# A second buffer for the softmax scales, GpSimd's scaling placed earlier, and V's last products placed earlier

## The chip, the cores and the metric

The kernel runs on one core of a Trainium2 chip. A core has a matrix engine (TensorE, PE in the profile; PEld is its weight load), a vector engine (VectorE, DVE), a scalar engine (ScalarE, ACT), a general engine (GpSimd, POOL) and an engine that mostly issues transfers (SyncE, SP). Each works through its own list of instructions in order and waits on semaphores. The metric is device time in microseconds; lower is better.

## The reference

One layer of a gated cross-attention block with a mixture of experts. B = 4 sequences of S = 512 tokens, width 256, 16 heads of 16:

```python
x = x + jnp.tanh(g_xattn[0]) * _L0_xattn_ref(_layernorm(x, axis=-1), ctx_1024, ctx_1024, ...)
x = x + jnp.tanh(g_ffn[0]) * _L0_ffn_ref(_layernorm(x, axis=-1), ...)
```

```python
q = _split_heads(Q @ Wq.T + bq)
k = _split_heads(K @ Wk.T + bk)
v = _split_heads(V @ Wv.T + bv)
scores = jnp.einsum('bhqd,bhkd->bhqk', q, k) * scale
attn = jax.nn.softmax(scores, axis=-1)
ctx = jnp.einsum('bhqk,bhkd->bhqd', attn, v)
...
return ctx @ Wo.T + bo
```

The second half (`_L0_ffn_ref`) routes every token to the 2 best of 8 experts, adds a shared expert, and is not touched by the change.

## The kernel before

**Attention in groups.** Attention runs over 16 groups (`GROUPS`): a group `i` is one sequence and four heads. A group has four steps (`kt`, 128 keys each). In a step TensorE makes four score tiles (`scores`, line 1621), four tiles of scores for the row maxima of a later group (`scores_for_max`, line 1387), and the products of the weights with V for the step before (`values`, line 1500). ScalarE takes the exponentials (line 816) and copies the products out (`sums_copy`, line 802). VectorE reduces the maxima (line 939). GpSimd adds the four partial sums of a group (`add_part`, line 679, three per group).

**How a group gets its maxima.** The row maxima are subtracted inside the score product, as extra rows of `QS`. For group i+1 they are finished in the first step of group i. Then GpSimd splits them (`split_max`, lines 589 and 591), VectorE transposes them (line 947), GpSimd copies them (`max_rows`, line 602, semaphore `m_ready`), and SyncE loads them (`load_max`, line 404, `QK<-mparts` in the rows). TensorE can't begin group i+1 before that load has landed (`m_in`).

**SyncE's list.** SyncE works in passes; pass i goes with group i. It issues `load_group(i+3)`: twelve transfers of 64 KB (lines 394 and 397) with the queries and keys of a later group. The first four wait until group i-1's scores are done, the other eight wait until the first step of group i has its exponentials (`exp_done`). Then come `load_max(i+1)`, `load_sums(i-1)` (line 409), `store_scale(i-2)` (line 413) and `load_scale(i-3)` (line 420). After pass 12 there is no `load_group`; in passes 12 to 14 weights of the second half follow.

**The scales.** For the first 14 groups the softmax division works on the transposed context: denominators go out by `load_sums`, VectorE takes reciprocals, `store_scale` writes them to memory and `load_scale` reads them back, each row repeated 16 times, into `SCALES` (the space of V's weights, `w_v` in the rows). One `SCALES` buffer holds two groups, and GpSimd multiplies two groups of context by it at once (`scale_context(n)`, line 633, for groups 2n and 2n+1, semaphore `ctx_scaled`). `load_scale(i)` waits until `ctx_scaled` reaches i // 2, so the pair before must have been multiplied.

**GpSimd's list.** In its iteration i: the last addition of group i-1, `split_max(i+1)`, `max_rows(i+1)`, `pack_out(i-1)` (four transfers, line 354), an addition of a bias to one tile of X (line 668), the first addition of group i, in odd iterations from 5 on `scale_context((i-5)//2)`, and the second addition of group i. It reaches these about a third of a group to a whole group after TensorE began group i.

**The first steps.** V of the last sequence is made inside the first two steps of group 0: `last_value_rows(kt, 0)` after the first pair of maxima tiles and `last_value_rows(kt, 1)` after the second pair (line 1485), and ScalarE copies it out after the fourth exponential of the step (`v_copy`, line 733). The score tiles, V's products and the sums share four banks in turn, so the score tile four turns after a V tile waits for that copy.

Of the kernel before, what the change touches and what calls it, by code (L numbers as in the profile page):

```python
# [6 lines left out]
ALU = mybir.AluOpType  # L7
# [8 lines left out]
def flamingo_layer(nc, x, ctxT, g_xattn, g_ffn, WqT, bq, WkT, bk, WvT, bv, WoT, bo,  # L16
# [3 lines left out]
    DK = D // H  # L20
# [46 lines left out]
    with ExitStack() as stack:  # L67
# [65 lines left out]
        SCALE = sb("SCALE", [P, 2, G * TB])  # L133
        SCALES = W["v"][:, :, :].rearrange("p c d -> p (c d)")
        CTX = CH[:, :, :].rearrange("p t d -> p (t d)")[:, 24:24 + TURNED // 2 * S].rearrange("p (n s) -> p n s", s=S)
# [89 lines left out]
        den_in, scale_out = sems("den_in", 2), sems("scale_out", 2)  # L225
        scale_ready, scale_in, ctx_scaled = sem("scale_ready"), sems("scale_in", 2), sem("ctx_scaled")

# [129 lines left out]
        def _(sp):  # L357
# [57 lines left out]
            def load_scale(i):  # L415
                sp.wait_ge(scale_out[i % 2], times(i))
                if i == 0:
                    sp.wait_ge(v_done, 2 * B)
                wait(sp, ctx_scaled, i // 2)
                sp.dma_start(SCALES[64 * (i % 2):64 * (i % 2 + 1), :],  # L420
                             r_scr[i].unsqueeze(1).to_broadcast([G, DK, S])).then_inc(scale_in[i % 2], 16)

# [119 lines left out]
        def _(pool):  # L542
# [85 lines left out]
            def scale_context(n):  # L628

                for h in range(2):  # L630
                    pool.wait_ge(ctx_in[h], 16 * G * (n + 1))
                    pool.wait_ge(scale_in[h], 16 * (n + 1))
                nc.gpsimd.tensor_tensor(CTX[:, n, :], CTX[:, n, :], SCALES, ALU.mult).then_inc(ctx_scaled, 1)

# [46 lines left out]
            for i in range(TURNED + 1):  # L681
                if i:
                    add_part(i - 1, 3)
                split_max(i + 1)
                max_rows(i + 1)
                if i:
                    pack_out(i - 1)
                else:
                    bias_x(range(4))
                if i < 12:  # L690
                    bias_x(range(4 + i, 5 + i))
                add_part(i, 1)
                if i >= 5 and i % 2:
                    scale_context((i - 5) // 2)
                if i < TURNED:
                    add_part(i, 2)
# [26 lines left out]
        def _(act):  # L723
# [84 lines left out]
            for i in range(GROUPS):  # L808
                for kt in range(TB):
                    for j in range(G):  # L810
                        act.wait_ge(st_done[j % 2], G // 2 * (TB * i + kt) + j // 2 + 1)
                        if i:
                            act.wait_ge(pv_done, TB * (i - 1) + kt + 1)
                        if i == 0 and kt == 2 and j == 2:
                            act.wait_ge(v_done, 2 * B)
                        nc.scalar.activation(PT[:, kt, j, :], PS[:, ring_bank("score", TB * i + kt, j), :], ACT.Exp).then_inc(exp_done, 1)  # L816
                        n = TB * i + kt - TAIL
                        if j == 3 and n in (2, 4):
                            h2t_first(n // 2 - 1)
                    if i == 0 and kt < 2:  # L820
                        v_copy(B - 1, PS[:, ring_bank("v", kt), :], kt)
                    if TB * i + kt:
# [531 lines left out]
        def _(pe):  # L1354
# [250 lines left out]
            for i in range(GROUPS):  # L1605
# [18 lines left out]
                for kt in range(TB):  # L1624
                    pairs = pairs_at(i, kt)
                    scores(kt, 0)
                    scores(kt, 1)
                    for n in pairs[0:1]:
                        scores_for_max(n)
                        scores_for_max(n + 1)  # L1630
                    if i == 0 and kt < 2:
                        last_value_rows(kt, 0)
                    scores(kt, 2)
# [235 lines left out]
```

## Time and profile before

| | |
|---|---|
| median of 3 runs | 471.99 us (471.62 to 473.8) |
| the profiled execution | 474.82 us, of which the span of the profile is 472.6 us |
| TensorE busy | 440.2 us (93%) |
| VectorE busy | 315.0 us (67%) |
| ScalarE busy | 267.2 us (57%) |
| GpSimd busy | 223.1 us (47%) |

Times in the rows are microseconds from the start of the span. 2.2 us of the profiled execution lie outside the span. A busy TensorE is not TensorE at its full rate; the granted clock (PEclk) is 1.00 at 2.4 GHz and 0.50 at 1.2 GHz.

### The profile page before, as it was taken

To read this page: it belongs to the slowest core of one execution; us is meant where nothing else is said; L and a number is where in the kernel's file an instruction comes from. 1 tells how busy PE (TensorE), PEld (TensorE's weight loads), DVE (VectorE), ACT (ScalarE), POOL (GpSimd) and SP (SyncE) were. 2 spreads that over 40 slices of the span, in tenths; PEclk is the share of its full clock that TensorE was granted. 3 is DMA by queue.
4 is the path that set the end of the run, shared out by engine and by line. 5 is a ranking of instruction groups with operands and counts; after the bars stand their busy time and mean duration, and the time that the engine had idled before them with its cause. 6 is when DMAs were issued, how large, how long until landed. Compare 5 with 4: busy or idle time off the path is not lost.

```text
span 472.6 us, 8388 instructions
## 1 busy us (share of the span) xinstructions
PE 440.2 (93%) x2294; PEld 225.8 (48%) x2294; DVE 315.0 (67%) x719; ACT 267.2 (57%) x564; POOL 223.1 (47%) x345
## 2 busy tenths in 40 slices
PE   8999999999969979495999999999999999999997
PEld 7654444333323323132355464575555555555745
DVE  1976938999866959394837877555665656542574
ACT  2545439999977959395864611113666667631110
POOL 5335525877863939384654476750333233322000
PEclk9999969999997989798999999999999999999999
DMA  8689561334362434327082582241323223211931
GB/s 259 242 238 295 172 234 53 90 97 106 84 115 64 89 89 82 76 65 144 19 242 86 157 289 91 101 121 49 90 81 91 83 88 91 81 56 48 359 112 60
DMA packets 45500, 58.93 MB, mean 125 GB/s; under 512 B 12496, under 2 KB 25680, under 8 KB 45456
## 3 DMA queue, kind: packets, MB, share of 16 engines
q1 hardware_dynamic: 38864, 46.05, 35.0%
q0 software_dynamic: 4960, 10.53, 7.1%
q10 hardware_dynamic: 1632, 1.84, 1.2%
q8 instruction: 19, 0.31, 0.3%
q14 instruction: 25, 0.20, 0.2%
HBM read 36.35 MB, written 19.81 MB: 119 GB/s over the span
## 4 chain that ended last, share of the span: by engine, by line
PE 64%; ACT 8%; DMA 8%; DVE 7%; issue 7%; SPq 6%; POOL 0%; ACTq 0%; DVEq 0%; POOLq 0%
PE PS L1665 11%; PE PS L1776 9%; ACT R L816 7%; PE PS L1500 6%; DMA QK<-mparts 6%; PE PS L1678 6%; PE PS L1621 5%; PE PS L1795 5%; PE PS L1440 4%; PE PS L1387 4%; PE PS L1771 3%; PE PS L1547 3%; SPq L397 2%; SPq L394 2%; PE PS L1790 2%
## 5 line engine op out<-in xcount | busy, mean ns | idle before, releaser
L939 DVE TENSOR_REDUCE nmax<-PS 128x2 f32<-128x1024 f32 x114 | 134.2, 1214 | 42.0 <-PE PS L1387 40.5
L816 ACT ACTIVATE R<-PS 128x512 f32<-128x512 f32 x256 | 134.3, 630 | 37.3 <-PE PS L1621 36.8
L1621 PE MATMUL PS<-QK 50*128 50x512 f32 x256 | 84.1, 475 | 22.5 <-DMA QK<-mparts 21.2
L679 POOL TENSOR_TENSOR R<-R 128x512 f32<-128x512 f32 x48 | 61.6, 1284 | 43.6 <-ACT R L802 42.0
L1621 PEld LDWEIGHTS PS<-QK 50*128 50x128 f32 x256 | 37.4, 197 | 83.4 <-ACT R L816 38.7
L1500 PE MATMUL PS<-R 128*32 128x512 f32 x512 | 72.6, 639 | 2.5 <-ACT R L816 1.6
L718 POOL DMA_INDIRECT token_y<-R,dest x34 | 32.6, 959 | 86.7 <-DVE R L1270 86.4
L1387 PE MATMUL PS<-QK 48*128 48x512 f32 x256 | 61.6, 458 | 1.3 <-DVE nmax L925 0.9
L1776 PE MATMUL PS<-R 128*128 x100 | 47.3, 595 | 0.2 <-ACT R L884 0.2
L831 ACT ACTIVATE R<-PS 128x512 f32<-128x512 f32 x16 | 9.6, 597 | 60.6 <-PE PS L1665 60.6
L802 ACT COPY R<-PS 128x512 f32<-128x512 f32 x64 | 38.6, 603 | 7.5 <-PE PS L1500 7.0
L1387 PEld LDWEIGHTS PS<-QK 48*128 48x128 f32 x256 | 29.3, 200 | 22.1 <-DVE nmax L939 13.1
L640 POOL DMA_INDIRECT slot_x<-CH,pos x32 | 31.1, 973 | 10.8 <-issue 8.4
L1308 DVE TENSOR_TENSOR R<-R,PS 128x256 f32<-128x256 f32 x34 | 14.3, 421 | 32.4 <-ACT R L881 27.2
L1665 PE MATMUL PS<-R,wgate 128*128 128x512 f32 x64 | 30.4, 597 | 0.0
L1665 PE MATMUL PS<-R,wup 128*128 128x512 f32 x64 | 30.3, 595 | 0.0
L881 ACT ACTIVATE R<-PS 128x256 f32<-128x256 f32 x34 | 13.0, 383 | 30.1 <-PE PS L1776 27.3
L354 POOL DMA_DIRECT2D CH<-R x56 | 27.8, 501 | 4.2 <-POOL mparts L602 4.2
L1678 PE MATMUL PS<-wdown,R 128*128 128x256 f32 x128 | 28.9, 380 | 0.0
L1678 PEld LDWEIGHTS PS<-wdown,R 128*128 128x128 f32 x128 | 24.0, 190 | 4.4 <-issue 1.4
L1776 PEld LDWEIGHTS PS<-R 128*128 128x128 f32 x100 | 18.7, 190 | 14.3 <-issue 13.1
L1795 PE MATMUL PS<-fc,R 128*128 x100 | 25.6, 380 | 0.0
(181 smaller groups left out, 621.5 us busy)
## 6 DMA issues: line engine op xcount, KB each, us to landing
QK<-q_parts SPq DMA_DIRECT2D x96, 64.0 KB, 2.8
QK<-k_parts SPq DMA_DIRECT2D x96, 64.0 KB, 2.9
k_parts<-R SPq DMA_DIRECT2D x8, 512.0 KB, 4.0
q_parts<-R SPq DMA_DIRECT2D x8, 512.0 KB, 4.8
R<-in_fc_w_dram SPq DMA_DIRECT2D x16, 256.0 KB, 5.1
R<-token_y SPq DMA_DIRECT2D x4, 1024.0 KB, 9.1
R<-slot_x SPq DMA_DIRECT2D x25, 129.0 KB, 2.1
fc<-in_fc_w_dram SPq DMA_DIRECT2D x16, 128.0 KB
```

What stands on the lines that cost most here:

```text
L679: nc.gpsimd.tensor_tensor(OT[i % 2], OT[i % 2], PART[kt - 1], ALU.add).then_inc(summed, 1)
L718: nc.gpsimd.indirect_dma_start(token_y, bass.IndirectOffsetOnAxis(ap=dest[:, j:j + 1], axis=0), YE[:, j % UN, :], None).then_inc(y_out[j % ...
L802: nc.scalar.copy(PART[kt - 1] if kt else OT[i % 2], PS[:, ring_bank("sums", n), :]).then_inc(sums_out, 1)
L816: nc.scalar.activation(PT[:, kt, j, :], PS[:, ring_bank("score", TB * i + kt, j), :], ACT.Exp).then_inc(exp_done, 1)
L939: nc.vector.tensor_reduce(nmax[:, i % 2, at:G * TB:G * TB // 2], PS[:, smax_bank(n):smax_bank(n) + 2, :], AX.X, ALU.max, negate=True).then ...
L1387: mm(PS[:, smax_bank(n), :], QS[g][at, h, qt * P:(qt + 1) * P], KST[g][at, h, :], start=True, stop=True).then_inc(smax_done[n % 2], 1)
L1500: last = mm(PS[32 * j:32 * j + VW, ring_bank("sums", n), :], VA[:, b * TB + kt, (g * G + j) * VS:(g * G + j) * VS + VW], PT[:, kt, j, :], ...
L1621: mm(PS[:, ring_bank("score", TB * i + kt, j), :], KST[g][at, h, kt * P:(kt + 1) * P], QS[g][at, h, :], start=True, stop=True).then_inc(st ...
L1665: last = mm(PS[:, gu_bank(n, k), :], w[:, d, c * P:(c + 1) * P], H2T[:, d, b * S:(b + 1) * S], start=(d == 0), stop=(d == DC - 1))
L1678: last = mm(PS[:, down_bank(b, t), half * D:(half + 1) * D], HS[:, b % 2, c, t * P:(t + 1) * P], wdown[:, c, :], start=(c == 0 and half == ...
L1776: last = mm(PS[:, 1 + u, :], XGT[:, u, c * P:(c + 1) * P], fc1[:, c, e, :], start=(c == 0), stop=(c == DC - 1))
L1795: last = mm(PS[:, 5 + u, 0:D], HET[:, u, c * P:(c + 1) * P], fc2[:, c, e, :], start=(c == 0), stop=(c == IE // P - 1))
```

## The change

Three edits. `SCALES` becomes two buffers, the space of V's weights and that of Q's weights, used in turn by pairs of groups; `load_scale(i)` waits for one pair less (`ctx_scaled` at i // 2 - 1) and once for Q's last product; `scale_in` has four semaphores. GpSimd's `scale_context` stands ahead of the bias addition and of `add_part(i, 1)`. In the first two steps of group 0, V's first products stand ahead of the first pair of maxima tiles, and ScalarE's copy of V stands ahead of the fourth exponential.

```diff
-        SCALES = W["v"][:, :, :].rearrange("p c d -> p (c d)")
+        SCALES = [W[n][:, :, :].rearrange("p c d -> p (c d)") for n in "vq"]
...
                 sp.wait_ge(scale_out[i % 2], times(i))
                 if i == 0:
                     sp.wait_ge(v_done, 2 * B)
-                wait(sp, ctx_scaled, i // 2)
-                sp.dma_start(SCALES[64 * (i % 2):64 * (i % 2 + 1), :],
-                             r_scr[i].unsqueeze(1).to_broadcast([G, DK, S])).then_inc(scale_in[i % 2], 16)
+                if i == 2:
+                    sp.wait_ge(qk_done, 4 * B)
+                wait(sp, ctx_scaled, i // 2 - 1)
+                sp.dma_start(SCALES[i // 2 % 2][64 * (i % 2):64 * (i % 2 + 1), :],
+                             r_scr[i].unsqueeze(1).to_broadcast([G, DK, S])).then_inc(scale_in[i % 4], 16)
...
-                    pool.wait_ge(scale_in[h], 16 * (n + 1))
-                nc.gpsimd.tensor_tensor(CTX[:, n, :], CTX[:, n, :], SCALES, ALU.mult).then_inc(ctx_scaled, 1)
+                    pool.wait_ge(scale_in[2 * (n % 2) + h], 16 * (n // 2 + 1))
+                nc.gpsimd.tensor_tensor(CTX[:, n, :], CTX[:, n, :], SCALES[n % 2], ALU.mult).then_inc(ctx_scaled, 1)
...
+                if i >= 5 and i % 2:
+                    scale_context((i - 5) // 2)
                 if i < 12:
                     bias_x(range(4 + i, 5 + i))
                 add_part(i, 1)
-                if i >= 5 and i % 2:
-                    scale_context((i - 5) // 2)
...
                     for j in range(G):
+                        if i == 0 and kt < 2 and j == 3:
+                            v_copy(B - 1, PS[:, ring_bank("v", kt), :], kt)
...
-                    if i == 0 and kt < 2:
-                        v_copy(B - 1, PS[:, ring_bank("v", kt), :], kt)
...
                     scores(kt, 1)
+                    if i == 0 and kt < 2:
+                        last_value_rows(kt, 0)
                     for n in pairs[0:1]:
                         scores_for_max(n)
                         scores_for_max(n + 1)
-                    if i == 0 and kt < 2:
-                        last_value_rows(kt, 0)
```

SyncE's list at the end of pass 5, with the waits in brackets (`o_scales` is the memory that holds the scales, `w_v` and `w_q` are the two buffers). Before:

```order
L404 DMA QK<-mparts 2x8x128
L409 DMA DENS<-R 128x1x16 [waits summed]
L413 DMA o_scales<-SCALE 128x16 [waits scale_ready]
L420 DMA w_v<-o_scales 64x1x512 [waits ctx_scaled,scale_out0]
L394 DMA QK<-q_parts 16x2x512 [waits st_done1,st_done0]
```

and after:

```order
L404 DMA QK<-mparts 2x8x128
L409 DMA DENS<-R 128x1x16 [waits summed]
L413 DMA o_scales<-SCALE 128x16 [waits scale_ready]
L422 DMA w_q<-o_scales 64x1x512 [waits qk_done,scale_out0]
L394 DMA QK<-q_parts 16x2x512 [waits st_done1,st_done0]
```

No transfer has moved in SyncE's list; the load of the scales no longer waits for GpSimd there.

GpSimd's list in its iteration 5, from the copies of the maxima on. Before:

```order
L602 COPY mparts<-mturned 32x32 x4
L354 DMA CH<-R 16x512 x4
L668 TENSOR_TENSOR X<-X,tg_bo 128x256
L679 TENSOR_TENSOR R<-R 128x512
L633 TENSOR_TENSOR CH<-CH,w_v 128x512
L679 TENSOR_TENSOR R<-R 128x512 x2
L589 CAST nmax_parts<-nmax 128x16
```

and after:

```order
L604 COPY mparts<-mturned 32x32 x4
L354 DMA CH<-R 16x512 x4
L635 TENSOR_TENSOR CH<-CH,w_v 128x512
L670 TENSOR_TENSOR X<-X,tg_bo 128x256
L681 TENSOR_TENSOR R<-R 128x512 x3
L591 CAST nmax_parts<-nmax 128x16
```

The multiplication has moved ahead of the bias addition and of one addition; nothing was added to the iteration.

TensorE's list in the first two steps of group 0 (1621 or 1623 are scores, 1387 or 1389 maxima tiles, 1485 or 1487 V). Before:

```order
L1621 MATMUL PS<-QK 128x512 x2
L1387 MATMUL PS<-QK 128x512 x2
L1485 MATMUL PS<-w_v,R 128x256 x2
L1621 MATMUL PS<-QK 128x512
L1387 MATMUL PS<-QK 128x512 x2
L1485 MATMUL PS<-w_v,R 128x256 x2
L1621 MATMUL PS<-QK 128x512 x3
L1387 MATMUL PS<-QK 128x512 x2
L1485 MATMUL PS<-w_v,R 128x256 x2
L1621 MATMUL PS<-QK 128x512
```

and after:

```order
L1623 MATMUL PS<-QK 128x512 x2
L1487 MATMUL PS<-w_v,R 128x256 x2
L1389 MATMUL PS<-QK 128x512 x2
L1623 MATMUL PS<-QK 128x512
L1389 MATMUL PS<-QK 128x512 x2
L1487 MATMUL PS<-w_v,R 128x256 x2
L1623 MATMUL PS<-QK 128x512 x3
L1487 MATMUL PS<-w_v,R 128x256 x2
L1389 MATMUL PS<-QK 128x512 x2
L1623 MATMUL PS<-QK 128x512
```

In both steps the first V products have changed places with the first pair of maxima tiles.

## Rows read from the trace of the kernel before

**Rows 1.** Page, part 4: shares of the chain that ended last, by line.

```profile
PE PS L1665 11%; PE PS L1776 9%; ACT R L816 7%; PE PS L1500 6%; DMA QK<-mparts 6%; PE PS L1678 6%; PE PS L1621 5%; PE PS L1795 5%; PE PS L1440 4%; PE PS L1387 4%; PE PS L1771 3%; PE PS L1547 3%; SPq L397 2%; SPq L394 2%; PE PS L1790 2%
```

**Rows 2.** Waits: who waited for whom, us in total, times, longest; SyncE's own last.

```profile
PE PS L1621 <- DMA QK<-mparts: 21.2, 6, 5.9
SPq L250 <- POOL CH L633: 13.9, 5, 3.2
```

**Rows 3.** Timeline of TensorE, first score tiles of groups 6, 7, 9, 11, 13.

```profile
127.79 0.51 PE L1621 MATMUL PS<-QK 50*128 50x512 f32 x2 [0.88 <-DMA QK<-mparts]
142.65 0.79 PE L1621 MATMUL PS<-QK 50*128 50x512 f32 x2 [4.81 <-DMA QK<-mparts]
168.46 0.55 PE L1621 MATMUL PS<-QK 50*128 50x512 f32 x2 [3.91 <-DMA QK<-mparts]
195.55 0.79 PE L1621 MATMUL PS<-QK 50*128 50x512 f32 x2 [5.94 <-DMA QK<-mparts]
222.19 0.80 PE L1621 MATMUL PS<-QK 50*128 50x512 f32 x2 [5.26 <-DMA QK<-mparts]
```

**Rows 4.** Windows: groups 0; 1 to 5; 7; 6 to 13; half clock; 5.

```profile
core 0: us, PE busy (x) PEld busy (x) DVE busy (x) ACT busy (x) POOL busy (x), PEclk, DMA share, GB/s
56.30:76.49 20.19, 18.12 (x74) 7.94 (x71) 11.29 (x13) 11.15 (x22) 7.24 (x13) 0.75 0.45 152
76.49:127.79 51.30, 49.64 (x324) 19.00 (x321) 48.47 (x50) 50.60 (x102) 38.57 (x70) 1.00 0.39 99
142.65:154.48 11.83, 11.83 (x64) 4.55 (x64) 8.93 (x10) 9.62 (x19) 5.19 (x13) 0.76 0.26 67
127.79:233.78 105.99, 85.56 (x512) 32.41 (x512) 75.85 (x80) 80.01 (x159) 64.22 (x115) 0.89 0.41 83
62.90:73.20 10.30, 10.30 (x35) 4.62 (x36) 3.34 (x4) 4.22 (x9) 4.27 (x9) 0.50 0.60 219
116.85:127.79 10.94, 9.97 (x68) 3.86 (x65) 10.11 (x11) 10.62 (x22) 8.61 (x15) 1.00 0.42 101
```

**Rows 5.** Timeline of SyncE in passes 3 and 4 (no wait for `ctx_scaled`).

```profile
105.90 0.56 SPq L420 DMA_DIRECT2D w_v<-o_scales  x1
113.63 1.12 SPq L404 DMA_DIRECT2D QK<-mparts  x2
```

**Rows 6.** Timeline of SyncE in passes 5 and 7 to 8.

```profile
121.51 1.96 SPq L394 DMA_DIRECT2D QK<-q_parts  x1
...
153.21 0.48 SPq L413 DMA_DIRECT2D o_scales<-SCALE  x1
157.00 0.56 SPq L420 DMA_DIRECT2D w_v<-o_scales  x1
...
163.23 1.11 SPq L404 DMA_DIRECT2D QK<-mparts  x2
```

**Rows 7.** The chain that ended last, in order of time: start, us, what.

```profile
125.50 2.24 DMA QK<-mparts
136.01 6.59 DMA QK<-mparts
163.81 4.60 DMA QK<-mparts
```

**Rows 8.** Timeline of GpSimd: iterations 5, 5 to 6, 8, and its last multiplication.

```profile
127.84 1.27 POOL L633 TENSOR_TENSOR CH<-CH,w_v 128x512 f32<-128x512 f32 x1
...
130.94 1.30 POOL L679 TENSOR_TENSOR R<-R 128x512 f32<-128x512 f32 x1 [0.58 <-ACT R L802]
...
160.35 0.98 POOL L602 COPY mparts<-mturned 32x32 f32<-32x32 f32 x4 [0.31 <-DVE mturned L947]
...
264.83 1.28 POOL L633 TENSOR_TENSOR CH<-CH,w_v 128x512 f32<-128x512 f32 x1 [6.87 <-DMA w_v<-o_scales]
```

**Rows 9.** Timeline of group 0's first two steps: TensorE's two idle times.

```profile
57.65 0.50 PE L1387 MATMUL PS<-QK 48*128 48x512 f32 x2 [0.91 <-DVE nmax L925]
...
62.52 0.50 PE L1621 MATMUL PS<-QK 50*128 50x512 f32 x1 [1.16 <-ACT R L733]
```

More of the change, by code:

```diff
@@ L225, in flamingo_layer @@
         den_in, scale_out = sems("den_in", 2), sems("scale_out", 2)
-        scale_ready, scale_in, ctx_scaled = sem("scale_ready"), sems("scale_in", 2), sem("ctx_scaled")
+        scale_ready, scale_in, ctx_scaled = sem("scale_ready"), sems("scale_in", 4), sem("ctx_scaled")
         ct_t, wo_done, x1_ready = (sem(n) for n in ("ct_t", "wo_done", "x1_ready"))
```

## The prediction

> **What bounds the kernel now.** First the chain that ended last, summed by line [rows 1]: TensorE has most of it, but 6% of the span stands under the load of a group's maxima, and 6% of 472.6 is 28 us in which no engine computes on the chain. Next the waits [rows 2]: TensorE's score product waited 21.2 us for that load, in 6 waits, and SyncE itself was held for 13.9 us, in 5 waits, by GpSimd's multiplication with the scales. Then TensorE's timeline shows where [rows 3]: 0.88 us at group 6, then 4.81, 3.91, 5.94 and 5.26 us at groups 7, 9, 11 and 13, together 19.92 us for the last four. Every second group stalls, and GpSimd multiplies in every second of its iterations. Last the windows [rows 4]: groups 1 to 5 took 51.30 us, 10.26 each; groups 6 to 13 took 105.99 us. A group without a stall takes 142.65 - 4.81 - 127.79 = 10.05 us [rows 3]. So eight groups cost 105.99 - 8 x 10.05 = 25.6 us over their smooth time: 19.92 us of stalls, and 5.7 us that lie in the groups after them. Group 7 shows what these are: 11.83 us, TensorE busy throughout, at a mean granted clock of 0.76, after its 4.81 us of idleness [rows 3, 4].
>
> **Why every second group stalls.** In passes 3 and 4 SyncE's load of the scales goes out at once; the load of the maxima follows at 113.63, 7.7 us later [rows 5], and group 5 starts without a stall. In pass 7 the scales are ready to load at 153.69 but go out at 157.00, 3.3 us late, because the one buffer is still to be multiplied [rows 6]. Behind that load stand the twelve transfers of the next group and then the next maxima. GpSimd had these maxima ready at 160.35 + 0.98 = 161.33 [rows 8]; SyncE issued them at 163.23 [rows 6], 1.9 us late. Worse, they then landed 4.60 us after their second issue at 163.81, and the ones of group 7 took 6.59, where those of group 6 took 2.24 [rows 7]. The two slow ones were queued behind a load of scales and twelve transfers issued back to back; in passes 3 to 5 the twelve were broken in two by SyncE's wait for the exponentials, which there was a real wait.
>
> **Part 1, the second buffer.** It takes the wait for `ctx_scaled` from SyncE, five times, 13.9 us of SyncE's time. What is next there? The first four transfers wait for the scores of the group before, which are done as a group starts, and the other eight for the first exponentials, as in passes 3 to 5. In pass 8 SyncE had 1.9 us too much and was held 3.3 us, so the maxima go out when GpSimd has them, at 161.33 in the times of before. The second issue is 0.58 later (163.81 against 163.23), and the landing takes 2.24 to 6.59 by the rows; I take 2.24, since what stands ahead is then what stood ahead of group 6's load. That gives 164.15. TensorE was ready at 168.46 - 3.91 = 164.55. So the stall goes, with only 0.4 us to spare, and with it the fallen clock. The load of the scales itself comes 3.3 us earlier and nothing waits for it until GpSimd's next multiplication. The new wait for Q's last product, once, costs nothing: that product was issued before attention began. A group can't go under 10.05 us for another reason: VectorE is busy 48.47 of 51.30 us in groups 1 to 5, ScalarE 50.60 [rows 4].
>
> With so little to spare, not every stall goes. SyncE's issues hang now and then (1.96 us for one at 121.51 [rows 6], where group 6 then came 0.88 us late [rows 3]). Groups 1 to 5 have such hitches in them, so I use their 10.26 us as the length: 8 x 10.26 = 82.1 us. At the ends: 8 x 10.05 = 80.4, and 8 x 10.94 = 87.5, if all were like group 5, the worst of the five [rows 4].
>
> **Part 2, GpSimd's order.** The multiplication costs 1.27 us as before [rows 8]; only its place changes, some 2 us earlier (a bias addition and one of the additions of 1.3 us). Behind it stand the bias addition and the additions of the group, and behind those the next split of the maxima. The sum of GpSimd's work to that split is the same. In iteration 5 GpSimd still had 0.58 us of idleness before the last addition at 130.94 [rows 8], but group 6 was 0.88 us late; without that, GpSimd is 0.88 - 0.58 = 0.3 us behind in each second group. This now matters, as the maxima's way has only 0.4 us to spare. I charge 0.3 us four times, 1.2 us; the ends are 0 and 4 x 1.27 = 5.1. It can't gain: SyncE no longer waits for the multiplication.
>
> Parts 1 and 2 together: 82.1 + 1.2 = 83.3 us for groups 6 to 13 in place of 105.99, a gain of 22.7.
>
> **Part 3, V's products in group 0.** TensorE was idle 0.91 us before a pair of maxima tiles, waiting for VectorE, and 1.16 us before a score tile, waiting for ScalarE's copy of V, which stands behind the fourth exponential [rows 9]. V's products now stand in the first hole, and the copy comes before that exponential. The first hole is filled, 0.9 us; of the second I take half, 0.5, since the copy still waits for the second V products. Gain 1.4 us, at most 2.1. Moving the maxima tiles behind two V products delays VectorE by up to 1.1 us; it is idle for 8.9 of the 20.19 us of this stretch [rows 4], which hides it. If that cover were gone, this part would lose 1.1.
>
> **Sum.** 22.7 + 1.4 = 24.1 us. The profiled execution took 474.82 us, so 450.7 for a like one; it stood 2.8 us above the median of 471.99. The rest, from group 14 on, is TensorE's list and moves up whole: the weights loaded in passes 12 to 14 are issued behind the maxima, so they delay none of the groups here, and SyncE's last loads wait on the end of attention as before. Predicted median: 471.99 - 24.1 = 447.9 us.
>
> **Rivals.**
>
> *The clock stays up in group 0.* The granted clock was 0.50 from 62.90 to 73.20, with TensorE busy for all 10.30 us [rows 4], after a stretch with the two holes of [rows 9]. With the holes filled it may not fall. Full clock halves at most that: 5.1 us; ScalarE and VectorE would take part of it back, so 4: 444. The holes are only 2.1 us of the stretch before, which speaks against it. Chance 0.08.
>
> *The slow landings stay.* If the 4.6 to 6.6 us come from a loaded memory and not from what is queued ahead, SyncE's earlier issue is all that is won: 1.9 us at groups 9, 11 and 13 each and 1 us at group 7, 6.7 us, plus 1.4 at the start: 463.9. The trace speaks against it with 2.24 us in a pass with the same transfers. The Trainium skill, page "DMA: Bandwidth & Descriptors", section "Latency and other measured facts", gives memory access as 0.2 us on average and 2 us at high load; by that the long landings are the load's and would stay. Chance 0.11.
>
> *GpSimd becomes the bound.* With the stalls gone it has no idle time in which to catch up, and the multiplication shows in full, 5.1 us in place of 1.2, plus hitches: 452. Chance 0.12.
>
> *SyncE is held by something else.* If the wait for the scores or for `scale_out` ends as late as the one removed, nothing goes: 471. In passes 3 and 4 neither did. Chance 0.02.
>
> *Slower.* The multiplication now stands ahead of two additions and, behind them, the maxima. If its scales have not landed, all of GpSimd's list waits. The last multiplication of before waited 6.87 us for its load [rows 8]. Five such waits are 34 us against the 24 won: 482. The point at which it starts is a landing later than 10 us, since the second load of a pair goes out a pass ahead of its use (105.90 for the first [rows 5], one pass later for the second, and use at 127.84 - 2.0 [rows 8]); it outweighs the gain from about 5 us above that. The longest landing in the rows is 6.59. Chance 0.02.
>
> **How the numbers follow.** The forecast has what is left, 0.65, with its own range: 80.4 to 87.5 us for eight groups, 0 to 2.1 us at the start and 0 to 5.1 for GpSimd, not all at their ends, so 445 to 453. The range that should hold 8 in 10 takes in the clock's rival and GpSimd's and part of the way to the slow landings: 443.5 to 459. Left out are the slow landings, SyncE's and the slower case, 0.15. About 0.5% (2.4 us) is what a measurement of this kernel can tell from no change. Faster by more: all but the last two rivals and a rest, 0.95; within it 0.03; slower 0.02.
>
> **What would show it.** SyncE's wait for GpSimd's multiplication is gone from the waits, and the wait of the score product for the maxima falls from 21.2 us to under 4. Groups 7, 9, 11 and 13 start within 1 us of the end of the group before, groups 6 to 13 take 81 to 88 us at a mean granted clock of 1.00, and group 0 takes 18 to 19 us in place of 20.19. The loads of the maxima land in about 2.2 us. Wrong would be: landings of 4 us and more with SyncE not held, or a GpSimd without idle time and late splits.

## The result and the profile after

The changed kernel takes 442.64 us (median of 6 executions, 441.38 to 444.28); the kernel before, measured beside it, 470.90 (468.99 to 473.80). The ratio is 0.940, 95% interval [0.936, 0.943]: 6% faster. The forecast of 447.9 was 5.3 us too high, and the range from 443.5 to 459 just misses the time.

The profiled execution of the changed kernel took 441.38 us, with a span of 439.6. First its chain that ended last, summed by engine and by line; this answers to [rows 1].

```profile
PE 89%; DVE 6%; issue 3%; ACT 1%; POOL 0%; DVEq 0%; ACTq 0%; POOLq 0%
PE PS L1502 12%; PE PS L1667 11%; PE PS L1623 10%; PE PS L1778 10%; PE PS L1389 8%; PE PS L1442 7%; PE PS L1680 6%; PE PS L1797 5%; PE PS L1773 4%; PE PS L1549 3%; DVE nmax L941 3%; PE PS L1420 2%; PE PS L1792 2%; PE PS L1752 2%; PE PS L1760 2%
```

The load of the maxima (`QK<-mparts`), 6% before, is gone from the chain, and SyncE with it. The row of the score product among the costliest groups (busy time, mean ns | idle time before it) says the same: 0.4 us of idleness in all, where the load alone had cost 21.2 [rows 2].

```profile
L1623 PE MATMUL PS<-QK 50*128 50x512 f32 x256 | 80.4, 447 | 0.4 <-ACT R L735 0.2
```

In the waits of the changed kernel, SyncE's wait for GpSimd's multiplication (13.9 us in [rows 2]) has no row any more. What is left for SyncE in attention is waiting for work that isn't there yet (us in total, times, longest):

```profile
SPq L404 <- POOL mparts L604: 15.3, 15, 5.0
SPq L394 <- ACT R L820: 13.1, 12, 1.8
```

Then the windows, which answer to [rows 4]: group 0, groups 1 to 5, groups 6 to 13, and from group 14 to the end.

```profile
core 0: us, PE busy (x) PEld busy (x) DVE busy (x) ACT busy (x) POOL busy (x), PEclk, DMA share, GB/s
56.36:70.92 14.56, 14.11 (x75) 6.56 (x72) 11.26 (x13) 10.93 (x22) 6.59 (x13) 1.00 0.65 211
70.92:120.82 49.90, 49.58 (x325) 19.09 (x322) 47.87 (x50) 49.76 (x101) 38.31 (x70) 1.00 0.42 102
120.82:200.80 79.98, 79.27 (x517) 30.81 (x514) 76.75 (x81) 79.62 (x161) 65.81 (x116) 1.00 0.47 110
200.80:439.60 238.80, 232.11 (x1186) 133.77 (x1182) 142.69 (x492) 100.72 (x241) 85.81 (x96) 1.00 0.37 117
```

The two profiled executions differ by 472.6 - 439.6 = 33.0 us of span:

| stretch | before | after | difference | forecast |
|---|---|---|---|---|
| group 0 | 20.15 | 14.56 | -5.6 | -1.4 |
| groups 1 to 5 | 51.30 | 49.90 | -1.4 | 0 |
| groups 6 to 13 | 105.99 | 79.98 | -26.0 | -22.7 |
| group 14 to the end | 238.82 | 238.80 | 0.0 | 0 |

Every group from 1 to 13 now takes 9.9 to 10.0 us, and in the 79.98 us of groups 6 to 13 ScalarE is busy for 79.62 and TensorE for 79.27. No engine waits there for a load of maxima any more; which of the two full engines sets the 10.0 us wasn't tested. SyncE's timeline around group 9's maxima shows the new pass (in the kernel before, [rows 6] has the same pass):

```profile
139.97 0.56 SPq L422 DMA_DIRECT2D w_v<-o_scales  x1
140.63 0.40 SPq L394 DMA_DIRECT2D QK<-q_parts  x1
...
142.01 0.42 SPq L397 DMA_DIRECT2D QK<-k_parts  x1
143.52 0.30 SPq L394 DMA_DIRECT2D QK<-q_parts  x1
...
146.67 0.42 SPq L397 DMA_DIRECT2D QK<-k_parts  x1
147.73 1.11 SPq L404 DMA_DIRECT2D QK<-mparts  x2
```

The load of the scales goes out at once. Four transfers follow, then 1.1 us of waiting for exponentials (142.43 to 143.52), then eight more, and then a wait for the maxima: 147.09 to 147.73. GpSimd's copy of the maxima was ready at 146.73 + 0.97 = 147.70, and SyncE issued their load 0.03 us later:

```profile
146.73 0.97 POOL L604 COPY mparts<-mturned 32x32 f32<-32x32 f32 x4 [0.31 <-DVE mturned L949]
```

The second issue was at 148.31; group 9 started at 150.80, so the load landed in at most 2.5 us.

### The profile page after: what moved, and what is told of

It is laid out like the page before. It is cut to its first block, busy times and chain, and to the rows that moved or that the text cites. A ratio compares the mean times of both kernels' runs of the same rounds, so it can differ in the third digit from the quotient of the medians.

```text
span 439.6 us, 8387 instructions
## 1 busy us (share of the span) xinstructions
PE 430.1 (98%) x2294; PEld 223.4 (51%) x2294; DVE 315.3 (72%) x719; ACT 265.5 (60%) x564; POOL 223.5 (51%) x345
## 4 chain that ended last, share of the span: by engine, by line
PE 89%; DVE 6%; issue 3%; ACT 1%; POOL 0%; DVEq 0%; ACTq 0%; POOLq 0%
PE PS L1502 12%; PE PS L1667 11%; PE PS L1623 10%; PE PS L1778 10%; PE PS L1389 8%; PE PS L1442 7%; PE PS L1680 6%; PE PS L1797 5%; PE PS L1773 4%; PE PS L1549 3%; DVE nmax L941 3%; PE PS L1420 2%; PE PS L1792 2%; PE PS L1752 2%; PE PS L1760 2%
## 5 line engine op out<-in xcount | busy, mean ns | idle before, releaser
L1623 PE MATMUL PS<-QK 50*128 50x512 f32 x256 | 80.4, 447 | 0.4 <-ACT R L735 0.2
L1502 PE MATMUL PS<-R 128*32 128x512 f32 x512 | 68.2, 603 | 2.5 <-ACT R L820 1.6
L1623 PEld LDWEIGHTS PS<-QK 50*128 50x128 f32 x256 | 34.7, 184 | 55.7 <-ACT R L820 35.6
L1389 PE MATMUL PS<-QK 48*128 48x512 f32 x256 | 56.9, 436 | 0.8
L1389 PEld LDWEIGHTS PS<-QK 48*128 48x128 f32 x256 | 24.6, 185 | 22.2 <-DVE nmax L941 13.5
```

The source lines that it names most:

```text
L1389: mm(PS[:, smax_bank(n), :], QS[g][at, h, qt * P:(qt + 1) * P], KST[g][at, h, :], start=True, stop=True).then_inc(smax_done[n % 2], 1)
L1502: last = mm(PS[32 * j:32 * j + VW, ring_bank("sums", n), :], VA[:, b * TB + kt, (g * G + j) * VS:(g * G + j) * VS + VW], PT[:, kt, j, :], ...
L1623: mm(PS[:, ring_bank("score", TB * i + kt, j), :], KST[g][at, h, kt * P:(kt + 1) * P], QS[g][at, h, :], start=True, stop=True).then_inc(st ...
```

## Experiments

Group starts are those of the group's first score tile. "Landing" is the time from the second issue of a maxima load to the start of the group that waits for it; it is a bound from above where the group didn't wait.

### The three parts, one at a time

**Part 3 alone** on the kernel before (the last two hunks of the change's diff, ScalarE's copy and V's products):

```diff
+                        if i == 0 and kt < 2 and j == 3:
+                            v_copy(B - 1, PS[:, ring_bank("v", kt), :], kt)
...
                     scores(kt, 1)
+                    if i == 0 and kt < 2:
+                        last_value_rows(kt, 0)
```

> The kernel before with the third edit alone (V's products and ScalarE's copy earlier in group 0). If the edit itself keeps the granted clock of TensorE up, group 0 goes from 20.2 to about 14.6 us, the stalls at groups 7, 9, 11 and 13 stay, and the time falls by 5 to 6 us. If the clock in the changed kernel stayed up by luck or through the other edits, group 0 gives 1 to 2 us and the clock falls as before.

Measured: 469.01 us against 472.73 for before on the same chip, 3.7 us less, where 5 to 6 was expected; ratio 0.993 [0.989, 0.997]. Group 0 took 14.57 us, at a clock of 1.00. The stalls stayed, at groups 7, 9, 11 and 13; the first three of them:

```profile
137.39 0.80 PE L1621 MATMUL PS<-QK 50*128 50x512 f32 x2 [6.32 <-DMA QK<-mparts]
164.76 0.80 PE L1621 MATMUL PS<-QK 50*128 50x512 f32 x2 [6.03 <-DMA QK<-mparts]
191.69 0.79 PE L1621 MATMUL PS<-QK 50*128 50x512 f32 x2 [5.66 <-DMA QK<-mparts]
```

**Part 1 alone** (the second buffer):

```diff
+        SCALES = [W[n][:, :, :].rearrange("p c d -> p (c d)") for n in "vq"]
...
-                wait(sp, ctx_scaled, i // 2)
+                wait(sp, ctx_scaled, i // 2 - 1)
```

> The kernel before with the second buffer alone. If SyncE's wait for GpSimd's multiplication is what makes every second group stall, groups 6 to 13 go from 106.0 to 80 to 83 us and the time falls by 23 to 27 us, with GpSimd's order as it was. If the earlier place of the multiplication matters too, some of the stalls stay: under 20 us of gain.

Measured: 446.13 us against 472.73 for before on the same chip, ratio 0.945 [0.936, 0.954]. So the buffer alone brings 26.6 us. Groups 6 to 13 took 83.7 us, a little over the 80 to 83 expected. One stall of size was left, at group 7: SyncE was on time, but the landing took 4.95 us. The scale load had gone out at once, and the twelve transfers were broken in two, though by only 0.7 us (125.84 to 126.51). Groups 9 to 13 took 10.0 us each.

```profile
123.39 0.55 SPq L422 DMA_DIRECT2D w_q<-o_scales  x1
...
125.42 0.42 SPq L397 DMA_DIRECT2D QK<-k_parts  x1
126.51 0.30 SPq L394 DMA_DIRECT2D QK<-q_parts  x1
...
130.58 1.12 SPq L404 DMA_DIRECT2D QK<-mparts  x2
```

```profile
136.12 0.59 PE L1623 MATMUL PS<-QK 50*128 50x512 f32 x2 [2.17 <-DMA QK<-mparts]
```

**Part 2 alone** (GpSimd multiplies ahead of the additions, one buffer):

```diff
+                if i >= 5 and i % 2:
+                    scale_context((i - 5) // 2)
                 if i < 12:
                     bias_x(range(4 + i, 5 + i))
                 add_part(i, 1)
-                if i >= 5 and i % 2:
-                    scale_context((i - 5) // 2)
```

> The kernel before with GpSimd's multiplication earlier, and one buffer. SyncE's wait ends about 2 us sooner (3.3 to 1.3 us). If what stalls TensorE is mainly twelve transfers that are issued without a break, 2 us are nearly enough: two or more of the four stalls go or shrink to under 2 us, 8 to 20 us of gain. If the load of the scales must not wait at all, the stalls stay at 4 us and more: under 5 us of gain. If this order delays the maxima, it is slower.

Measured: 457.69 us, ratio 0.969 [0.960, 0.977], so 15.0 us. The trace is of the longest of its four executions (462.23 us). It separates two things that the prediction had side by side, SyncE's lateness and the slow landing. The multiplication is earlier, so SyncE's wait is shorter:

```profile
125.84 0.47 SPq L413 DMA_DIRECT2D o_scales<-SCALE  x1
127.68 0.55 SPq L420 DMA_DIRECT2D w_v<-o_scales  x1
...
133.43 0.42 SPq L397 DMA_DIRECT2D QK<-k_parts  x1
134.19 1.13 SPq L404 DMA_DIRECT2D QK<-mparts  x2
```

SyncE lost 1.4 us (126.31 to 127.68), but was at the maxima at 133.85 and waited for them until 134.19. It was late for no maxima in this execution, and still groups 7, 9, 11 and 13 stalled for 2.71, 3.57, 2.15 and 1.36 us, with landings of 5.25, 6.05, 4.62 and 3.84 us. The wait of 1.4 us had used up the pause among the twelve transfers, which now follow the load of the scales without one. The slow landing is a cost of its own, beside SyncE's lateness.

**All but part 2** (the changed kernel with GpSimd's order as before, the diff above the other way round):

> The changed kernel with GpSimd's old order. With two buffers nobody waits for the multiplication, and the sum of GpSimd's work up to the split of the maxima is the same: same time as the changed kernel within 0.5%. If the order does matter with two buffers, it is slower by 1 us or more.

Measured: 442.76 us (441.72 to 443.79, 4 executions), ratio 0.939 [0.932, 0.946], against 442.64 and 0.940 for the whole change. Groups 6 to 13 took 80.15 us with the old order and 79.98 with the new. So with two buffers GpSimd's order makes no difference that these runs can tell (the two intervals leave room for some 3 us in the whole time, the groups for about 0.2).

The parts fit together: 26.6 for the buffer and 3.7 for the first steps is 30.3 us, against 30.0 for the two together on that chip (472.73 - 442.76). Part 2's 15.0 us are a part of the buffer's, not an addition to them.

### What makes a landing slow

The prediction's reason was the scale load with twelve transfers behind it, back to back. Three runs take it apart. In the first the kernel before loads 8 KB of scales in place of 128 KB; it leaves most of the scales out, so its result is wrong.

```diff
-                sp.dma_start(SCALES[64 * (i % 2):64 * (i % 2 + 1), :],
-                             r_scr[i].unsqueeze(1).to_broadcast([G, DK, S])).then_inc(scale_in[i % 2], 16)
+                sp.dma_start(SCALES[64 * (i % 2):64 * (i % 2) + G, :], r_scr[i]).then_inc(scale_in[i % 2], 16)
```

> The kernel before with the load of the scales cut from 64 rows (128 KB) to 4 rows (8 KB); so most of the scales are not loaded. SyncE still waits for GpSimd. If the 128 KB are what slows the load of the maxima behind them, the four stalls fall to 1 to 2 us each. If the twelve transfers issued without a break are enough, the stalls shrink by about 1 us each and stay over 3 us, and the time stays within 6 us of before.

Measured: 467.43 us in one execution. SyncE was as unbroken as before, and 1.3 to 1.6 us late for the maxima, but they landed in 2.96, 3.06, 3.26 and 2.87 us. The stalls shrank to 1.80, 1.63, 1.78 and 1.46 us. One of them:

```profile
157.84 0.80 PE L1620 MATMUL PS<-QK 50*128 50x512 f32 x2 [1.63 <-DMA QK<-mparts]
```

In the second, the changed kernel holds all twelve transfers until the exponentials are done and issues them unbroken:

```diff
-                    load_group(i + 3, (0, 1))
                     sp.wait_ge(exp_done, G * (TB * i + 1))
-                    load_group(i + 3, range(2, UNIT))
+                    load_group(i + 3)
```

> The changed kernel, but all twelve transfers of a group wait for the first exponentials, so they go out without a break as in the stalled passes of before; SyncE never waits for GpSimd's multiplication. The maxima are then issued about 1.6 us later than in the changed kernel. If an unbroken queue of twelve is what makes their landing slow, it takes 4 to 6.6 us and groups 3 to 12 stall by 3 us and more each, 30 us or more over the changed kernel. If not, landings stay at 2.2 us and the stalls at about 1 us each, 10 us over it.

Measured: 461.75 us, some 19 us over the changed kernel where the expectation had 10 or over 30. Twelve unbroken transfers make SyncE late for most maxima (0.1 to 3.3 us), but the landings stayed at 1.8 to 3.2 us. So the unbroken twelve alone don't make a landing slow, and that half of the prediction's reason falls. Here, though, the scale load stood apart from them, with a pause of 2.9 us (129.01 to 131.87):

```profile
128.46 0.55 SPq L422 DMA_DIRECT2D w_q<-o_scales  x1
131.87 0.31 SPq L394 DMA_DIRECT2D QK<-q_parts  x1
...
137.40 1.11 SPq L404 DMA_DIRECT2D QK<-mparts  x2
```

In the third the same kernel issues the 128 KB load of the scales a pass later, right ahead of the twelve, with no pause between:

```diff
                     sp.wait_ge(exp_done, G * (TB * i + 1))
+                    if 0 <= i - 4 < TURNED:
+                        load_scale(i - 4)
                     load_group(i + 3)
...
-                if 0 <= i - 3 < TURNED:
+                if 0 <= i - 4 < TURNED and i + 3 >= GROUPS:
+                    load_scale(i - 4)
+                if i == GROUPS - 1:
                     load_scale(i - 3)
```

> As the run with unbroken transfers, but the load of the scales (128 KB) now goes out right ahead of the twelve, one pass later; GpSimd then finds its scales later too. In the run with unbroken transfers and the scales 8 us ahead, the maxima landed 1.8 to 3.2 us after their second issue. If it is the 128 KB together with the twelve, with no pause in SyncE's list, that makes the landing slow, it now takes 4 us and more in groups 4 to 12 and each of these groups stalls by 3 us and more: over 475 us. If the load of the scales only costs its place in the list, landings stay under 3.3 us and the time comes out within 8 us of the 461.8 of that run.

Measured: 498.44 us. The maxima of groups 5 to 13 now landed in 3.87 to 5.33 us, every one, where the run above had 1.76 to 3.19; in groups 2 to 4 of this run, before any scale load, it was 1.74 to 2.85. Groups 4 to 12 took 13.7 to 14.8 us. SyncE's rows of one pass, and the score tile that waited for its maxima:

```profile
138.29 0.54 SPq L422 DMA_DIRECT2D w_q<-o_scales  x1
138.94 0.40 SPq L394 DMA_DIRECT2D QK<-q_parts  x1
...
144.67 1.11 SPq L404 DMA_DIRECT2D QK<-mparts  x2
```

```profile
149.62 0.80 PE L1626 MATMUL PS<-QK 50*128 50x512 f32 x2 [3.90 <-DMA QK<-mparts]
```

So it takes both, 128 KB of scales and twelve transfers of 64 KB close behind it. A small load of scales brings the landing back to about 3 us, and so do pauses between, wherever they stand, if they are long enough. The time from the issue of the 128 KB to the second issue of the maxima shows how long. With no pause it is 6.8 us. Over all these runs the landing took 3.8 to 7.0 us where that time was 6.8 to 7.8 us, and under 3.5 us where it was 8.0 or more; the changed kernel has 8.05 to 8.37. So pauses of 1.2 us in sum were enough, and the 1.0 us at group 7 with part 1 alone (7.78 us) were not.

The trace also has a record of each packet that the transfers consist of, and these tell a load that is slow from a load that stands in a queue. The maxima are 32 packets of 512 bytes, the scales and the twelve transfers 448 packets of 2 KB:

| kernel, groups | first packet of the maxima, us after SyncE's first issue | longest packet of the maxima, us | last packet of scales and twelve, us after the second issue of the maxima |
|---|---|---|---|
| before, 7, 9, 11, 13 | 3.2 to 3.7 | 0.18 | 3.2 to 4.0 |
| changed, 5 to 13 | 1.2 to 1.3 | 0.23 | 0.3 to 1.6 |
| unbroken, scales ahead with a pause, 5 to 13 | 1.2 to 1.7 | 0.14 | 0.5 to 1.9 |
| unbroken, scales right ahead, 5 to 13 | 2.3 to 3.3 | 0.23 | 2.3 to 3.3 |

The maxima's own packets were short in all four kernels; in the slow passes they began late, while the transfers ahead were still under way. That decides against the rival by which the load itself is slow (it copies from one tile on the chip to another; only the transfers ahead of it read memory). One part of that rival stays open: the packets of the transfers ahead were longer too, 0.17 to 0.20 us in the mean (those behind the first 64) in the slow passes of before and 0.12 to 0.15 in the changed kernel, and whether the crowding makes them longer or their length the crowding, no run here separates.

The completion of a load comes later still: at group 7 of before the last packet of the maxima ended 4.46 us after the second issue and the completion came at 6.59, in group 8 of the changed kernel these were 1.74 and 2.13. This agrees with what the Trainium skill says on the page "DMA: Bandwidth & Descriptors", section "Queues, rings and completion order": the semaphore's increment lands only after every earlier write of its DMA engine.

### GpSimd's reserve

The changed kernel with two small operations on a scratch tile (0.45 us each) ahead of every multiplication:

```diff
             def scale_context(n):
 
+                nc.gpsimd.tensor_tensor(scratch[:, :], scratch[:, :], scratch[:, :], ALU.mult).then_inc(idle_work, 1)
+                pool.wait_ge(idle_work, 2 * n + 2)
+                nc.gpsimd.tensor_tensor(scratch[:, :], scratch[:, :], scratch[:, :], ALU.mult).then_inc(idle_work, 1)
+                pool.wait_ge(idle_work, 2 * n + 3)
```

> The changed kernel with two small GpSimd operations (about 1 us together) ahead of each multiplication with the scales, on a tile that nothing else uses. If GpSimd is about to become the bound, as one rival had it, groups 7, 9, 11 and 13 each start about 0.6 us late, 2 to 3 us in all. If it has a microsecond to spare, the group starts stay 10.0 us apart.

Measured: 447.28 us. The groups from 6 on took 11.71, 10.49, 11.12, 9.99, 10.96, 9.99, 11.00 and 9.99 us: about 1 us more for each pair, for about 1 us of added work (in the first pair the clock fell too, for 3.4 us from 131.3 on). No group waited for the load of its maxima, so the delay doesn't come in at the group starts, where the expectation had put it. It runs through VectorE, whose transposition of the maxima waited 4.6 us for GpSimd's split in groups 6 to 13, in 4 waits, and had no such wait in the changed kernel. In the iterations with a multiplication GpSimd has no idle time but two waits of 0.3 us inside its own steps:

```profile
142.52 0.45 POOL L636 TENSOR_TENSOR scratch<-scratch 128x160 f32<-128x160 f32 x1
143.04 0.45 POOL L638 TENSOR_TENSOR scratch<-scratch 128x160 f32<-128x160 f32 x1
143.58 1.29 POOL L643 TENSOR_TENSOR CH<-CH,w_q 128x512 f32<-128x512 f32 x1
144.82 0.73 POOL L678 TENSOR_TENSOR X<-X,tg_bo 128x256 f32<-128x256 f32 x1
145.52 4.14 POOL L689 TENSOR_TENSOR R<-R 128x512 f32<-128x512 f32 x3
149.60 0.20 POOL L595 CAST nmax_parts<-nmax 128x16 fp32r<-128x16 f32 x1
```

In the changed kernel an iteration with a multiplication is 10.15 us long (139.89 to 150.04), 0.15 more than a group; the next one has 0.62 and 0.78 us of idle time and makes up for it. Here are the rows of the full one:

```profile
139.89 1.27 POOL L635 TENSOR_TENSOR CH<-CH,w_q 128x512 f32<-128x512 f32 x1
141.12 0.73 POOL L670 TENSOR_TENSOR X<-X,tg_bo 128x256 f32<-128x256 f32 x1
141.82 4.15 POOL L681 TENSOR_TENSOR R<-R 128x512 f32<-128x512 f32 x3
145.92 0.20 POOL L591 CAST nmax_parts<-nmax 128x16 fp32r<-128x16 f32 x1
```

So GpSimd's list is full in every second group. That costs nothing yet, but one more microsecond in such an iteration costs a microsecond, as the run shows.

### Group 0 and its clock

TensorE's timeline of the changed kernel in group 0 answers to [rows 9]. The first hole is filled, and the second has shrunk from 1.16 to 0.24 us:

```profile
56.69 1.13 PE L1487 MATMUL PS<-w_v,R 128*128 128x256 f32 x4
57.75 0.51 PE L1389 MATMUL PS<-QK 48*128 48x512 f32 x2
...
61.09 0.50 PE L1623 MATMUL PS<-QK 50*128 50x512 f32 x1 [0.24 <-ACT R L735]
```

The granted clock stayed at 1.00, where [rows 4] have 0.50 from 62.90 on. Of the two moves in part 3, each was made alone on the kernel before, first V's products, then the copy:

```diff
                     scores(kt, 1)
+                    if i == 0 and kt < 2:
+                        last_value_rows(kt, 0)
```

> The kernel before with V's first products ahead of the maxima tiles on TensorE, and ScalarE's copy where it was. At 2.4 GHz I expect group 0 at 15.3 to 15.8 us (0.9 us of 16.25 gone with the first idle time), at a fallen clock 19 us.

```diff
                     for j in range(G):
+                        if i == 0 and kt < 2 and j == 3:
+                            v_copy(B - 1, PS[:, ring_bank("v", kt), :], kt)
```

> The kernel before with ScalarE's copy ahead of the fourth exponential, and V's products where they were. At 2.4 GHz I expect group 0 at 15.5 to 15.9 us (the second idle time shorter), at a fallen clock 19 us. If the two edits only work together, this one gives under 0.3 us.

Measured: with V's products alone moved the clock fell at 62.8, for 10.2 us, and group 0 took 19.65 us. With ScalarE's copy alone it stayed up and group 0 took 15.09, less than the 15.5 expected. A third kernel kept the old order and filled TensorE's two idle times with score products computed again:

```diff
+                    for _ in range({1: 4, 4: 5}.get(n, 0)):
+                        mm(PS[:, ring_bank("score", TB * i + kt, j), :], KST[g][at, h, kt * P:(kt + 1) * P], QS[g][at, h, :],
+                           start=True, stop=True)
```

> The kernel before, with nine score products of group 0 repeated (four times score tile 1 ahead of the first idle time of TensorE, five times tile 4 ahead of the second); the result is unchanged. V's products and the copy stay where they were. If the idle times let the clock fall in group 0, it now stays at 2.4 GHz and group 0 takes about 16.3 us, as in the one run of the old order in which the clock stayed up. If the clock falls there whatever TensorE does, group 0 takes 20 us.

Measured: clock up, group 0 at 16.22 us, stalls at groups 7, 9, 11 and 13 as before. That looked like a proof that the holes cause the fall, until the kernel before ran again:

> The kernel before once more, for the start of attention. So far the old order of group 0 was seen in four profiles: the clock fell in two (20.2 and 20.4 us) and stayed up in two (16.2 us). Either may come. Stalls of 4 to 6.6 us at groups 7, 9, 11 and 13, whatever the clock did in group 0.

Measured: 467.78 us, clock up all through group 0, which took 16.23 us, with both holes in it. So the old order doesn't always lose the clock, and one profile of each kernel can't tell; that holds for the three kernels above too, seen once each. To this question went the changed kernel with part 3 undone, the kernel before twice, and the changed kernel again.

> The changed kernel with V's products and ScalarE's copy in their old places, so parts 1 and 2 alone. If the order of the first steps is worth only its holes, group 0 takes 16.2 us, 1.7 more than in the changed kernel, and the median is 444.3. If the clock fell in this profile as it did in two of the five profiles of the old order, group 0 takes 20.2 and the profiled execution is at 448, while the median of the other executions lies between 444 and 448. If parts 1 and 2 had left something to be won by part 3 further on, the difference would be over 1.7 with the clock up.

> The kernel before once more, only for group 0. If the fall of the clock there is a matter of the execution, it comes in some profiles of this order and not in others: group 0 is 16.2 us or 20.2 us, nothing between. If it were the chip's doing, all profiles of this job agree. The stalls at groups 7, 9, 11 and 13 remain, 3.4 to 6.2 us each.

> As the one ahead: 16.2 or 20.2 us for group 0. With this one there are eight profiles of the old order; by the share so far (2 in 5) one of the three of this job shows the fall. If none does, the fall is rarer than it looked, and six of six for the new order says little.

> The changed kernel once more. Group 0 at 14.6 us with the clock at 1.00, as in six profiles of this order, if the new order keeps the clock up; 18.6 us if it only was lucky. Groups 1 to 13 at 10.0 us each, time 441 to 444.

Measured on this chip, where both kernels are 2% longer (before 481.31): 452.62 us for the change without part 3 (450.98 to 455.76; ratio 0.940 [0.933, 0.946]), 450.83 for the whole change in one execution. The clock fell in the profiles of the first three and not in that of the changed kernel. Group 0 took 18.99 us without part 3, 19.14 and 18.79 in the kernel before (481.90 and 484.42 us), and 14.55 in the changed one. So the expected "16.2 us or 20.2 us, nothing between" was wrong: here the clock was down for 6.8 us, where it had been 10.2. Without part 3 groups 6 to 13 took 80.03 us, so part 3 does nothing further on. The windows are those of 56.7 to 75.7 us and of 63.2 to 70.0; first the change without part 3, then the kernel before (the first of the two), then the whole change:

```profile
56.70:75.70 19.00, 16.85 (x76) 7.35 (x72) 11.47 (x13) 11.35 (x22) 7.25 (x13) 0.82 0.48 161
63.20:70.00 6.80, 6.80 (x23) 2.73 (x20) 2.57 (x3) 2.37 (x5) 2.51 (x7) 0.61 0.92 333
```

```profile
56.70:75.70 19.00, 16.86 (x72) 7.84 (x74) 11.31 (x13) 10.89 (x22) 7.25 (x13) 0.82 0.48 161
63.20:70.00 6.80, 6.80 (x20) 3.17 (x20) 2.57 (x3) 1.96 (x4) 1.94 (x6) 0.50 0.88 321
```

```profile
56.70:75.70 19.00, 18.56 (x104) 8.53 (x104) 15.38 (x16) 15.39 (x31) 9.58 (x15) 1.00 0.57 181
63.20:70.00 6.80, 6.71 (x41) 3.17 (x42) 5.16 (x6) 5.11 (x11) 3.51 (x8) 1.00 0.89 317
```

All profiles of group 0 together, without the three kernels that changed it in another way (V's products alone, the copy alone, the filled holes):

| order of the first steps | clock fell | clock stayed |
|---|---|---|
| old | 5 (18.8 to 20.4 us) | 3 (16.23 to 16.25 us) |
| new, both moves | 0 | 7 (14.54 to 14.58 us) |

If the order made no difference, all five falls among fifteen profiles would land on the eight of the old order in 56 of 3003 draws, 2%. So the new order most probably keeps the clock up. The chip may have a part in it: all three profiles of the old order on this last chip fell, and "all profiles of this job agree" had been named as the sign of that. It isn't the chip alone, since on another chip part 2 alone fell and part 1 alone didn't, both with the old order, and since the new order stayed up on the last chip too. What decides between the two outcomes of the old order wasn't found: the two holes of [rows 9], 0.91 and 1.16 us, stand in all eight profiles.

## Why the prediction was right and wrong

The stalls went for the reason given, but the gain was put too low. Two steps failed: the groups were sized too long (10.26 us each, and 1.2 us for GpSimd), and the fallen clock of group 0 was kept on both sides of the comparison.

**The mechanism of part 1: right, and one half of its explanation wrong.** The wait named went, nothing took its place, and the stalls of groups 7, 9, 11 and 13 went with it, also the fallen clock behind them. The scale load issued at once, the twelve in two pieces, the second issue at the time GpSimd allows and a landing of 2.5 to 2.7 us at most: all stand in the rows of after. "Queued behind a load of scales and twelve transfers issued back to back" was the right description; that the break inside the twelve is what matters was too narrow, since a pause ahead of the twelve does as well, and pauses of 1.0 us in sum were not enough at group 7 with part 1 alone.

**The length of a group: a step that failed, 2.1 us in groups 6 to 13.** The step was "groups 1 to 5 have such hitches in them, so I use their 10.26 us". Measured were 10.00. The hitch of group 6 in [rows 3] goes back to a single issue on SyncE that took 1.96 us [rows 6] in place of 0.42. Such hitches came elsewhere in other runs: waits of 0.19 and 0.21 us at groups 3 and 6 with part 1 alone, where SyncE was 0.6 to 0.7 us late, and of 0.71 at group 5 with part 2 undone, where SyncE was on time and the landing took 3.4 us. So they are none to three in a run and not one in each group, and they have more than one cause. The same step left groups 1 to 5 at 51.30 us on both sides; they took 49.90. The bound at the low end, 8 x 10.05, was the better value.

**GpSimd's 1.2 us: measured 0.** The step took "GpSimd is 0.3 us behind in each second group" from the difference of a hitch and an idle time. A full GpSimd just keeps up; the run with part 2 undone and the whole change differ by 0.1 us in the medians and by 0.2 in groups 6 to 13.

**Part 3: 1.4 us forecast, 1.7 measured** with the clock up on both sides (16.23 to 14.56). The two holes shrank by 0.91 and 0.92 us. The step "of the second I take half, 0.5" was too careful. ScalarE's copy alone gave 1.1 us (16.23 to 15.09), which was most of it.

**The clock in group 0: the other step that failed.** The rival had the right price, 4 us (18.8 to 20.4 us, less 16.2, is 2.6 to 4.2 us), and a chance of 0.08. The forecast kept the fall on both sides of the comparison, since "the holes are only 2.1 us of the stretch before". That argument weighed the holes by their size, with no row that showed the clock at 1.00 with the holes in it or out of it. One profile had shown one fall; it was read as a fixed property of the kernel, and it is a thing that comes in some executions.

**What would show it.** SyncE's wait is gone; the score product's wait for the maxima is gone as well, not just under 4 us. Groups 6 to 13 took 79.98 us at a clock of 1.00 where 81 to 88 was named, and group 0 took 14.56 where 18 to 19 was.

**Sum.** Against the profiled execution: 33.0 measured less 24.1 forecast is 8.9 us, made of 4.2 in group 0 (4 for the clock, and 0.3 for the order), 1.4 in groups 1 to 5, and 3.3 in groups 6 to 13 (2.1 for the length, 1.2 for GpSimd). Against the medians the miss is 5.3 us, and it divides otherwise. 1.1 of it is the start: the kernel before now measured 470.90, not 471.99. The rest is a gain of 28.3 in place of 24.1. On the chip where the parts ran alone, the second buffer was worth 26.3 us beside part 3 (469.01 - 442.76) where 22.7 was forecast, and part 3 was worth 3.7 where 1.4 was; so there the groups were 3.6 us too low and group 0 was 2.3 too low. The clock counts for less in a median than in the one profiled execution, since it falls in a part of the executions only; the larger miss is the length of the groups and GpSimd's charge.

**The other rivals.** Slow landings that stay: wrong, at most 2.5 to 2.7 us in the groups of after. SyncE held by something else: wrong, its waits for scores come to 2.1 us in four, none over 0.6. Slower by a multiplication that waits for its load: wrong; only the last one waited (6.9 us, as before), beyond the groups. GpSimd as the bound: wrong, but by less than 1 us of work in an iteration.

## What to carry to other kernels

A queue's held instruction costs twice: by its own lateness, and by taking away the pause that lets the transfers ahead of a latency-bound load drain. A second buffer removed both; an earlier consumer with one buffer removed the first, and left half of the stalls. And where the profile shows a fallen clock after short idle times, look at more than one execution before the fall is carried into both sides of a sum.

## What the runs showed of the hardware

- A small load that otherwise landed within 2.8 us, a few times within 3.4, took 3.8 to 7.0 us behind a 128 KB load and twelve of 64 KB issued 0.47 us apart without a pause, or with pauses of up to 1.0 us in sum. With the 8 KB load in front it took 2.9 to 3.3 us, and with a pause of some 3 us behind the 128 KB load 1.8 to 3.2. Its own packets took at most 0.3 us each either way; in the slow case they began 0.7 to 2.9 us later.
- SyncE's issue of a 64 KB transfer, 0.42 us, now and then takes 0.6 to 2.0 us, at a different place in each execution.
- The granted clock in a stretch with idle times of 0.91 and 1.16 us fell to 0.50 for 6.8 to 10.2 us in five executions and stayed at 1.00 in three of the same order. Without the first and with 0.24 us in place of the second it stayed at 1.00 in seven.
- From group 14 on the same list of work took 239 us in the profiles of some chips, and 8 to 16 us more in those of others, the kernel before and the changed one alike. What causes it wasn't looked for; it is why the comparisons of times here stay within one chip where they can, and else within the groups.
